# Attention over 32 heads: a hardware loop of four passes written out in a straight line

## The chip, the cores and the metric

The kernel runs on one core of a Trainium2 chip. The metric is the device time of one execution in microseconds (us), lower is better. A core has five engines that run their own instruction streams side by side and meet only at semaphores: TensorE (PE, matrix products), VectorE (DVE), ScalarE (ACT), GpSimd (POOL) and SyncE (SP, which here starts the transfers).

## The reference, cut to what matters

The reference is one decoder layer in float32: a state-space mixer, a grouped-query cross-attention over a context, a feed-forward part, each followed by a layer norm. Only the attention is touched:

```python
# b = 2, 16 heads in 4 groups, 512 queries, 1536 keys, head width 96
scores = jnp.einsum('bkgqd,bksd->bkgqs', q, k) * scale
attn = jax.nn.softmax(scores.astype(jnp.float32), axis=-1).astype(q.dtype)
out = jnp.einsum('bkgqs,bksd->bkgqd', attn, v)
```

## The kernel before, in words

The program has five phases, each with its own semaphores and buffers: `mamba_in`, `mamba_scan`, `project_norm_qkv`, `attention`, `attention_out_feed_forward`. A product in float32 is made of three matmuls on a high and a low part of each operand. q, k and v lie in DRAM when `attention` starts, and its result goes back to DRAM.

`attention` works through 2 x 16 = 32 heads (`hd`), in 8 groups of 4 heads that share k and v (`w` is the group, `g` the head in it, `s = w % 2` the buffer of k and v). In each head:

- PE makes 12 tiles of scores (`scores`, three matmuls each) of 128 keys by 512 queries into two PSUM banks in turn, so the scores of tile t wait for the exponential of tile t - 2. Between them it makes the products with v (`values`, three matmuls, four tiles behind, `LAG`), the products from which the next head's maxima are read (`maximum`, 4 x 3 matmuls), and at t = 10 four short transposes (`transposes`).
- ACT, for each tile, takes the exponential from PSUM (L1455) and copies it to the high part (L1458). At t = 6 it splits the query of the head after next (L1443), at six places of heads g = 1 and g = 2 it splits a piece of the next group's k or v (L1436, L1439), and at t = 10 it copies the row of maxima (L1448), once per head.
- POOL makes the low part of each exponential (L1552). DVE reduces the maxima (L1497), divides by the sums (L1504, L1510) and makes the low parts of q, k and v. SP loads k, v and q and stores the result.

All five engines run this through one helper, `heads` (L1383): a loop of `NW // 2 = 4` passes over a body in which 2 groups, 8 heads, are written out. Each engine has a loop of its own, with its own counter register `j`; no engine waits for another at the turn from one pass to the next. Inside the body every number that depends on the head, in a wait or in a transfer's address, is computed from `j`:

```python
        with eng.Fori(0, NW // 2) as j:
            for s in range(2):
                for g in range(G):
                    body(2 * G * j + G * s + g, 2 * j + s, g, s)
```

Before the loop, PE, ACT and DVE do the first head's maxima, its query and the first k and v; after it the last four tiles, the last division and the last store follow.

Of the kernel before, what the change touches and what calls it, by code (L numbers as in the profile page):

```python
# [34 lines left out]
G = NH // KV  # L35
# [1286 lines left out]
def attention(nc, res, d):  # L1322
# [18 lines left out]
    NW = B * KV  # L1341
# [40 lines left out]

    def heads(eng, body):  # L1383

        with eng.Fori(0, NW // 2) as j:
            for s in range(2):
                for g in range(G):
                    body(2 * G * j + G * s + g, 2 * j + s, g, s)

    SET, POOL_SET = 5, 2 + 2 * LAG  # L1390
    SPLIT_AT = ((1, 4), (1, 7), (1, 10), (2, 1), (2, 4), (2, 9))
# [1 line left out]
    with nc.Block() as block:  # L1393
        @block.sync
        def _(sp):
# [23 lines left out]
            sp.wait_ge(q_lo_done, 1)  # L1419
            load_q(2, 0)  # L1420
            heads(sp, body)
            store(NHD, 0)
            sp.wait_ge(on_st[0], 16 * (NHD // 2 + 1))
# [6 lines left out]
        def _(act):  # L1430
# [44 lines left out]
            row(0, 0)  # L1475
            act.wait_ge(before_done, 1)
            heads(act, body)

        @block.vector
        def _(dve):  # L1480
# [58 lines left out]
            maximum(0, 3)  # L1539
            queries(1, 1)  # L1540
            heads(dve, body)
            reciprocals(NHD, 0)
            divide(NHD, 0)
# [625 lines left out]
```

## Time and profile before

| | us |
|---|---|
| median of 3 runs (lowest, highest) | 3586.15 (3581.65, 3586.78) |
| profiled execution, its own time | 3582.83 |
| its span, first to last instruction | 3581.5 |
| the loop over heads in it, about | 1768 to 2422 |
| 41307 instructions; PE busy | 3221.2 (90%) |

The own time of the profiled execution is 1.3 us more than its span. The loop over heads is 654 us of the span, 18%. Its four passes can be told apart in the trace because ACT copies the row of maxima (L1448) once per head, and because the loop's own instructions stand under line 1385: a register operation at the head of each pass, and an addition and a compare-and-branch at its end.

### The profile page before, as it was taken

The numbers are of one execution on the slowest core, as the hardware profiler recorded it, in microseconds if no ns is written. First come the engines' busy times: TensorE is split into PE (matmuls) and PEld (weight loads), VectorE is DVE, ScalarE is ACT, GpSimd is POOL, SyncE is SP. The second block draws the span as 40 slices with busy tenths as digits, with TensorE's granted clock in tenths as the row PEclk, the third lists the DMA queues.
The fourth block names the chain that finished last, engine by engine and source line by source line (L and its number), as shares of the span: only waits on it lengthen the run. The fifth ranks groups of instructions, "written<-read, shape, count | busy, mean of one in ns | idle before, by whom it ended". The sixth has DMA issues, their size and how long they took to land. (4 is left out here: it accounts for less than half of the span.)

```text
span 3581.5 us, 41307 instructions
## 1 busy us (share of the span) xinstructions
PE 3221.2 (90%) x12763; PEld 2387.8 (67%) x12763; DVE 2195.0 (61%) x1925; ACT 1512.5 (42%) x2148; POOL 1399.2 (39%) x794
## 2 busy tenths in 40 slices
PE   9999777878777689999799999997889999999996
PEld 7877433333332267898587878786668888888884
DVE  6554499999999946621377777774644333333426
ACT  4447644444444432411387888782321122121111
POOL 0002299999999823000287878780100000000001
PEclk9999889999999999999899999999999999999998
DMA  3124531113110076422211111115211111111101
GB/s 110 41 80 165 184 128 62 45 50 139 50 62 31 15 252 208 144 80 94 76 32 32 35 31 35 31 33 199 78 65 47 41 59 53 35 53 53 47 18 59
DMA packets 125427, 273.15 MB, mean 76 GB/s; under 512 B 24448, under 2 KB 38656, under 8 KB 122400
## 3 DMA queue, kind: packets, MB, share of 16 engines
q1 hardware_dynamic: 107632, 262.42, 21.7%
q10 hardware_dynamic: 17712, 9.79, 0.9%
q8 instruction: 32, 0.52, 0.1%
q14 instruction: 51, 0.42, 0.0%
HBM read 207.87 MB, written 64.29 MB: 76 GB/s over the span
## 5 line engine op out<-in xcount | busy, mean ns | idle before, releaser
L799 PE MATMUL scan_ps_y<-scan_g,scan_ident 128*128 128x512 f32 x1024 | 518.8, 640 | 189.5 <-DVE scan_g L730 172.8
L771 POOL TENSOR_TENSOR scan_dbx<-scan_u,scan_b_bc 128x1024 f32<-128x1024 f32 x256 | 594.2, 2355 | 31.6 <-DMA scan_b_bc<-bc 31.6
L1552 POOL TENSOR_TENSOR at_p_lo<-at_p,at_p_hi 128x512 fp32r<-128x512 f32 x384 | 515.7, 1350 | 159.5 <-ACT at_p_hi L1458 149.1
L702 ACT ACTIVATE scan_ps_a<-scan_dt,scan_a_neg 128x512 f32<-128x512 f32 x512 | 328.0, 679 | 442.6 <-DVE scan_g L730 435.7
L799 PEld LDWEIGHTS scan_ps_y<-scan_g,scan_ident 128*128 128x128 f32 x1024 | 193.2, 199 | 482.5 <-DVE scan_g L730 296.0
L927 POOL TENSOR_TENSOR ff_y<-ff_y,ff_rstd 128x512 f32<-128x512 f32 x14 | 24.9, 1806 | 1124.1 <-DVE ff_rstd L916 1124.1
L743 DVE TENSOR_TENSOR_SCAN scan_ps_a<-scan_ps_a,scan_dbx 128x512 f32<-128x512 f32 x384 | 441.5, 1210 | 1.5 <-POOL scan_dbx L771 1.5
L1497 DVE TENSOR_REDUCE at_neg_max<-at_ps_mx 128x1 fp32r<-128x1536 f32 x132 | 232.0, 1758 | 164.3 <-PE at_ps_mx L1572 152.4
L1972 DVE TENSOR_TENSOR ff_hf<-ff_sg,ff_ps_u 128x1024 f32<-128x1024 f32 x28 | 34.2, 1221 | 388.2 <-PE ff_ps_u L97 388.2
L1455 ACT ACTIVATE at_p<-at_ps_s 128x512 f32<-128x512 f32 x384 | 227.8, 593 | 104.7 <-PE at_ps_s L1589 86.6
L1458 ACT ACTIVATE at_p_hi<-at_p 128x512 fp32r<-128x512 f32 x384 | 242.8, 632 | 12.2
L730 DVE TENSOR_TENSOR scan_g<-scan_ps_a,scan_c_bc 128x1024 f32<-128x1024 f32 x192 | 231.1, 1204 | 0.0
L95 PE MATMUL in_ps<-in_x_hi,in_w_hi 128*128 128x512 f32 x512 | 202.2, 395 | 0.0
L96 PE MATMUL in_ps<-in_x_lo,in_w_hi 128*128 128x512 f32 x512 | 200.7, 392 | 0.0
L97 PE MATMUL in_ps<-in_x_hi,in_w_lo 128*128 128x512 f32 x512 | 200.4, 391 | 0.0
L95 PE MATMUL ff_ps_g<-ff_x_hi,ff_w_hi 128*128 128x512 f32 x448 | 176.3, 394 | 5.7 <-DVE ff_x_lo L1912 5.7
L96 PE MATMUL ff_ps_g<-ff_x_lo,ff_w_hi 128*128 128x512 f32 x448 | 175.3, 391 | 0.0
L97 PE MATMUL ff_ps_g<-ff_x_hi,ff_w_lo 128*128 128x512 f32 x448 | 175.0, 391 | 0.0
L95 PE MATMUL ff_ps_u<-ff_x_hi,ff_w_hi 128*128 128x512 f32 x448 | 174.8, 390 | 0.0
L97 PE MATMUL ff_ps_y<-ff_h_hi,ff_w_lo 128*128 128x512 f32 x448 | 174.5, 389 | 0.0
L96 PE MATMUL ff_ps_y<-ff_h_lo,ff_w_hi 128*128 128x512 f32 x448 | 174.4, 389 | 0.0
L97 PE MATMUL ff_ps_u<-ff_x_hi,ff_w_lo 128*128 128x512 f32 x448 | 174.4, 389 | 0.0
(253 smaller groups left out, 7201.3 us busy)
## 6 DMA issues: line engine op xcount, KB each, us to landing
ff_w<-in_w SPq DMA_DIRECT2D x56, 512.0 KB, 4.2
in_w<-in_w_in SPq DMA_DIRECT2D x32, 512.0 KB, 3.6
mid_w<-in_w_out SPq DMA_DIRECT2D x32, 512.0 KB, 4.8
ff_w<-in_w SPq DMA_DIRECT2D x56, 256.0 KB, 2.6
ff_wo_wo<-in_w_o SPq DMA_DIRECT2D x32, 384.0 KB, 3.1
scan_cx<-in_ctx SPq DMA_DIRECT2D x9, 1024.0 KB, 5.7
sz<-in_xz SPq DMA_DIRECT2D x16, 512.0 KB, 3.0
dt<-in_acc SPq DMA_DIRECT2D x16, 512.0 KB, 3.6
```

Of the source, the lines that this page charges most:

```text
L95: nc.tensor.matmul(out, w_hi, x_hi, start=start, stop=False)
L96: nc.tensor.matmul(out, w_hi, x_lo, start=False, stop=False)
L97: return nc.tensor.matmul(out, w_lo, x_hi, start=False, stop=stop)
L702: nc.scalar.activation(ps_a[(2 * s + k) % SB][:, h], dt[s][:], ACT.Exp, scale=a_neg[:, it, 2 * k + h:2 * k + h + 1]).then_inc(a_ready, 1)
L730: nc.vector.tensor_tensor(g[s][:], ps_a[s][:], c_bc[:, 2 * k:2 * k + 2], ALU.mult).then_inc(g_ready, 1)
L743: nc.vector.tensor_tensor_scan(out[:, h], ps_a[slot][:, h], dbx[k % SL][:, h], 0.0, ALU.mult, ALU.add).then_inc(scanned, 1)
L771: nc.gpsimd.tensor_tensor(dbx[k % SL][:], u[s][:].unsqueeze(1).to_broadcast([P, 2, L]), b_bc[:, 2 * k:2 * k + 2], ALU.mult).then_inc(dbx_r ...
L799: last = nc.tensor.matmul(ps_y[:], ident[:], g[(2 * s + k) % SB][:, h], start=False, stop=k == NK - 1 and h == 1)
L1455: nc.scalar.activation(p[t % NSL][:], ps_s[t % 2][:], ACT.Exp, scale=SCALE).then_inc(exp_done, 1)
L1458: nc.scalar.activation(p_hi[t % NSL][:], p[t % NSL][:], ACT.Copy).then_inc(p_hi_done, 1)
L1497: nc.vector.tensor_reduce(neg_max[:, i, HD:HD + 1], ps_mx[:].rearrange("p n l -> p (n l)"), AX_X, ALU.max, negate=True).then_inc(max_done, 1)
L1552: nc.gpsimd.tensor_tensor(p_lo[t % NSL][:], p[t % NSL][:], f32(p_hi[t % NSL][:]), ALU.subtract).then_inc(p_lo_done, 1)
```

## The change

The helper `heads` no longer opens a loop. It calls the body 32 times, in the same order and with the same arguments as plain numbers; `s` is now `w % 2`. Nothing else is changed: the same data instructions in the same order on each engine, with the same semaphores and the same values waited for.

```diff
     def heads(eng, body):
 
-        with eng.Fori(0, NW // 2) as j:
-            for s in range(2):
-                for g in range(G):
-                    body(2 * G * j + G * s + g, 2 * j + s, g, s)
+        for w in range(NW):
+            for g in range(G):
+                body(G * w + g, w, g, w % 2)
 
     SET, POOL_SET = 5, 2 + 2 * LAG
```

## Rows read from the trace of the kernel before

**Rows 1.** The page: busy time and share of the span; the instruction queues (packets, MB, share).

```profile
PE 3221.2 (90%) x12763; PEld 2387.8 (67%) x12763; DVE 2195.0 (61%) x1925; ACT 1512.5 (42%) x2148; POOL 1399.2 (39%) x794
...
q8 instruction: 32, 0.52, 0.1%
q14 instruction: 51, 0.42, 0.0%
```

**Rows 2.** Windows, busy us: length, PE, PEld, DVE, ACT, POOL, then PE clock, DMA, GB/s.

```profile
1768.00:2422.00 654.00, 646.79 (x2828) 522.48 (x2828) 480.74 (x304) 525.48 (x884) 515.71 (x384) 0.99 0.12 33
```

**Rows 3.** Waits in 1768 to 2422: us in total, times, longest.

```profile
ACT L1455 <- issue: 8.5, 3, 3.3
...
PE at_ps_s L1587 <- ACT at_p L1455: 6.1, 3, 2.5
```

**Rows 4.** Timeline of the first turn, 1930 to 1937: start us, length, engine, line.

```profile
1930.91 0.63 ACT L1458 ACTIVATE at_p_hi<-at_p 128x512 fp32r<-128x512 f32 x1
1931.11 0.40 PE L1589 MATMUL at_ps_s<-at_q_hi,at_k_lo 96*128 96x512 f32 x1
...
1934.85 1.28 ACT L1455 ACT_TABLE_LOAD   x1 [3.31 <-issue]
1936.15 0.60 ACT L1455 ACTIVATE at_p<-at_ps_s 128x512 f32<-128x512 f32 x1
1936.78 0.63 ACT L1458 ACTIVATE at_p_hi<-at_p 128x512 fp32r<-128x512 f32 x1
...
1936.80 0.50 PE L1587 MATMUL at_ps_s<-at_q_hi,at_k_hi 97*128 97x512 f32 x1 [2.50 <-ACT at_p L1455]
```

**Rows 5.** Line 1385 in 1924 to 1938: sequencer, operation, ns, first and last start.

```profile
L1385 PEldq COMPARE_BRANCH  x1: 208/208/208, 1927.8 to 1927.8; - x1
L1385 PEldq FUSED_REGOPS  x1: 50/50/50, 1928.1 to 1928.1; - x1
...
L1385 ACTq COMPARE_BRANCH  x1: 45/45/45, 1931.0 to 1931.0; - x1
...
L1385 ACTq FUSED_REGOPS  x1: 66/66/66, 1934.7 to 1934.7; - x1
```

**Rows 6.** Line 281, the first phase's loop of 8 passes: operation, count, ns min/median/max.

```profile
L281 ACT ACT_TABLE_LOAD  x8: 1283/1283/1283, 28.3 to 200.3; - x8
```

**Rows 7.** Windows right behind the first and the second turn, columns as in Rows 2.

```profile
1937.00:1940.60 3.60, 3.60 (x10) 2.83 (x10) 0.02 (x1) 2.63 (x5) 3.11 (x3) 0.55 0.00 0
2100.20:2104.00 3.80, 3.80 (x17) 3.11 (x18) 1.52 (x1) 3.53 (x7) 3.21 (x3) 1.00 0.00 0
```

**Rows 8.** Timeline of PE at the second and the third turn.

```profile
2100.11 0.50 PE L1587 MATMUL at_ps_s<-at_q_hi,at_k_hi 97*128 97x512 f32 x1 [1.57 <-ACT at_p L1455]
...
2262.31 0.50 PE L1587 MATMUL at_ps_s<-at_q_hi,at_k_hi 97*128 97x512 f32 x1 [2.00 <-ACT at_p L1455]
```

**Rows 9.** Timeline of ACT, line 1448 of heads 0, 3, 4, 7, 8, 15, 16, 23, 24.

```profile
1789.63 0.59 ACT L1448 ACTIVATE at_q_hi<-at_ps_t 1x512 fp32r<-1x512 f32 x1
...
1849.70 0.59 ACT L1448 ACTIVATE at_q_hi<-at_ps_t 1x512 fp32r<-1x512 f32 x1
1869.60 0.59 ACT L1448 ACTIVATE at_q_hi<-at_ps_t 1x512 fp32r<-1x512 f32 x1
...
1929.66 0.59 ACT L1448 ACTIVATE at_q_hi<-at_ps_t 1x512 fp32r<-1x512 f32 x1
1953.89 0.59 ACT L1448 ACTIVATE at_q_hi<-at_ps_t 1x512 fp32r<-1x512 f32 x1
...
2093.90 0.59 ACT L1448 ACTIVATE at_q_hi<-at_ps_t 1x512 fp32r<-1x512 f32 x1
2115.64 0.59 ACT L1448 ACTIVATE at_q_hi<-at_ps_t 1x512 fp32r<-1x512 f32 x1
...
2255.64 0.59 ACT L1448 ACTIVATE at_q_hi<-at_ps_t 1x512 fp32r<-1x512 f32 x1
2277.84 0.59 ACT L1448 ACTIVATE at_q_hi<-at_ps_t 1x512 fp32r<-1x512 f32 x1
```

## The prediction

> **What bounds the kernel now.** I read the page first [rows 1]: PE is busy 90% of the span, no other engine over 61%, so a gain has to come out of time in which PE stands still or runs slow. The change touches only the loop over heads, so the second view is the windows for that stretch [rows 2]: in 654.0 us PE is busy 646.8, with the granted clock at 0.99 on the mean. PE is idle there for 7.2 us; that is nearly all that anything done to this loop can give back, beside what a slow clock costs.
>
> The third view is the waits of the same stretch [rows 3]. Of the 7.2 us, 6.1 are three waits of PE for the exponential on ACT, and ACT itself has three stretches, 8.5 us in all, in which it waits for nothing the profile shows ("issue"). Three is the number of turns of a loop of four passes.
>
> The fourth is the timeline of the first turn [rows 4]. The scores of the next tile are done on PE at 1931.11 + 0.40 = 1931.51, and ACT ends its last copy at 1930.91 + 0.63 = 1931.54, so the exponential could start at once. Instead ACT is idle for 3.31 us, then loads its activation table for 1.28 us, and the exponential starts at 1936.15: 4.6 us late. PE goes on with what it has, then stands 2.50 us for it, because the scores have two banks. The loop's own instructions say what the 3.31 us are [rows 5]: ACT's compare-and-branch is at 1931.0, the first instruction of the next pass at 1934.7, 3.7 us later. PE's branch (1927.8 to 1928.1) costs 0.3 us, while its engine still has matmuls queued.
>
> **The change part by part.**
>
> (1) *The turn of ACT goes*, three times: idle time of 8.5 us in all [rows 3] and no branch. The Trainium skill, "Runtime: NRT & Kernel Launch", section "Instruction fetch mechanics", says that a taken branch to a target outside the two pages held has to fetch it before going on, and that code in a row is fetched ahead, mostly hidden. The 3.7 against 0.3 us of [rows 5] fits that, if ACT's body doesn't fit and PE's does.
>
> (2) *Three of the four table loads go.* The exponential needs its table; inside a pass there is one load for 96 exponentials and 96 copies, so nothing in the body drives it out. The load is at the head of each pass because the state on entry isn't known there. The first phase shows the same rule: 8 passes, 8 loads [rows 6]. In a straight line only the first one is needed, and it lies beside PE's first scores already. That is 3 x 1.28 = 3.8 us of ACT.
>
> (3) *What PE gets back.* ACT's 8.5 + 3.8 = 12.3 us are not the sum, since PE has some cover. I take the sum from steps between equal points of successive heads [rows 9]. With no turn between them, head 3 to head 4 (the first of a group, like those behind a turn) takes 1869.60 - 1849.70 = 19.90 us. Across the turns it takes 24.23, 21.74 and 22.20. The excess is 4.33, 1.84 and 2.30 us, together 8.47.
>
> The parts agree with PE's side: its idle time is 2.50, 1.57 and 2.00 [rows 4, 8], 6.07 together, plus the start of the first matmul behind a gap. At the first turn there is one thing more: from 1937.0 to 1940.6 the granted clock is 0.55 and PE starts 10 matmuls in 3.6 us; behind the second turn it is 1.00 with 17 in 3.8 us [rows 7]. So behind the 2.50 us gap the clock fell to its 1.2 GHz level, behind 1.57 it stayed at 2.4. That costs 3.6 x 0.45 = 1.6 us and is inside the 4.33. With no gap there, it goes too.
>
> (4) *The turns of PE, DVE, POOL and SP go.* PE's costs 0.3 us of its sequencer [rows 5] and runs ahead of the matmuls. The scores that PE ends at 1931.51 [rows 4] belong to the next pass already, so PE is past its turn before ACT is; it is ACT that PE meets later. Price 0. Once ACT no longer stalls, next late would be POOL or DVE, but inside the passes they hold PE up nowhere that counts: 1.1 us is all PE's idle time outside the turns.
>
> (5) *Register arithmetic becomes constants.* Two waits and a computed value stand between an exponential and its copy, and the copy at 1936.78 starts 0.03 us behind the exponential's end (1936.15 + 0.60) [rows 4]. The arithmetic is done while the engine works. Lower bound of the gain 0; upper bound the 2.9 us worked out under rival C. I take 0, nearest to the 0.03 us row. A loss has no place: instructions only go away.
>
> (6) *More code is fetched*, once each, in place of a body that is run four times. Both instruction queues move 0.94 MB now, at 0.1% of the DMA engines [rows 1], beside a DMA share of 0.12 in the loop [rows 2]; bandwidth is no issue. Whether the fetch keeps ahead can be read off the first pass, which already runs all 8 heads as new code on all engines: heads 0 to 7 take 1929.66 - 1789.63 = 140.03 us there, and 2093.90 - 1953.89 = 140.01 and 2255.64 - 2115.64 = 140.00 in the second and third pass [rows 9], in which PE, DVE, POOL and SP run what they may still hold. New code costs 0.02 us per pass or nothing. Lower end 0; upper end, if each block were waited for, a turn's price of 1.84 to 4.33 us per stall. I take 0.
>
> (7) *Before and after the loop.* The first matmuls of the loop and the last tiles stay as they are; leaving the loop costs no jump. The last phase starts 8.5 us earlier as a whole. Price 0.
>
> **Sum.** 3582.83 - 8.47 = 3574.4 us for the profiled execution. Its time is 3.3 us below the median of the three runs, so for the median I expect 3586.15 - 8.47 = 3577.7, and say 3577. What one can tell from no change here is about 0.2%, 7.2 us; the forecast is only just over it, which is why "same" gets a good share.
>
> **The rivals.**
>
> *A. The fetch stays, only the loads go.* If ACT's buffer is refilled at the same rate in a straight line, it would meet a stall of some 3 us at three places anyway. Then 1.28 us per turn is taken off ACT, and PE's gaps of 2.50, 1.57 and 2.00 shrink by that much: 3.84, and 1.6 for the clock, since a gap of 1.2 is less than the 1.57 that left it alone. Gain 5.4 us at most, median 3581. For it: the idle is put down to no one. Against: the first pass crosses the same code with no such stall.
>
> The Trainium skill, "ScalarE: Activation LUTs", section "What ACT_TABLE_LOAD costs", gives a load 1283 ns, which the row has to the digit, and a drain of 1380 ns beside it. By that, part of the 3.31 us would be the load's and rival A would come out at 3 x 2.66 = 8.0 us off ACT, near the forecast.
>
> *B. A straight line that runs dry (slower).* Place: ACT, in front of an exponential, in the 24 heads of the passes that used to be repeats. ACT makes 884 / 32 = 28 operations a head [rows 2] with several waits beside each. Price: a stall of 3 us costs PE 1.84 to 4.33 us, mean 2.8. With one in each head: 24 x 2.8 = 67 us, less 8.5: 3645. It decides from 4 stalls on (4 x 2.8 = 11 > 8.5); to be slower by 0.2% it takes 6. Against: none in the 8 heads of the first pass.
>
> *C. The constants help as well.* The seven steps inside a pass take 140.03 us where seven of 19.90 would take 139.3 [rows 9]: 0.7 us a pass is lost in heads in which ACT has k and v to split beside its tiles. If register work is in that chain, up to 4 x 0.7 = 2.9 us more go: 3574.8. Against: the 0.03 us between ACT's operations [rows 4], which leaves next to nothing for it.
>
> *D. The loads aren't taken out*, or the loop is rebuilt in some way: ACT would be late by 1.28 us at most, about what PE's banks cover. Gain about 6 to 8.5 us; it ends inside the forecast's range.
>
> **How the numbers follow.** Forecast with D 0.78 (gain 6.5 to 10.5, median 3575.6 to 3579.7, plus some 2 us for the median of few runs); A 0.10; C 0.08; B 0.04. Faster by over 0.2% needs 3579.0 or less: most of the forecast (0.64 of its 0.78) and C: 0.72. Same: the rest of the forecast, and A: 0.24. Slower: B, 0.04. Range 3570 to 3584: C and the lower runs below, A and the higher runs above; B is left out.
>
> **What would show it.** In the profile after: one table load on L1455 in place of four; no "issue" idle time on ACT; no wait of PE for ACT's exponential over 0.5 us; steps across the old turns of 19.9 us; granted clock 1.00 at heads 8 and 9; seven steps inside a group of 8 heads of 140.0 us, as before; more MB on the instruction queues. New "issue" time on ACT or PE in the later heads would show A or B, seven steps well below 140.0 us C. The prediction is wrong if the steps come down and the total doesn't: something behind the loop would then have taken the time.

## The result, and the profile after

The changed kernel takes 3569.72 us (median of 5 runs, 3568.72 to 3573.32) against 3586.15 (5 runs timed beside it), so the two medians differ by 16.4 us. The ratio of the comparison, which isn't the quotient of the two medians, is 0.9959, 95% interval 0.9945 to 0.9974, that is 14.7 us less (9.3 to 19.7); gains "by the ratio" below are worked out in the same way. The direction is as forecast. The size is not: 8.5 us were forecast, and the median lies just under the range's low end of 3570. The profiled execution went from 3582.83 to 3573.32 us, 9.5 less, so profile and timed runs disagree by 5 us or more on the gain. Some 2 us of that disagreement turned out to be the lesson of this case; the rest stays open.

The page after, to be held against [rows 1]: the same matmuls, about as busy, and more code on one of the instruction queues.

```profile
PE 3217.1 (90%) x12763; PEld 2386.3 (67%) x12763; DVE 2197.4 (62%) x1925; ACT 1509.4 (42%) x2145; POOL 1400.5 (39%) x794
...
q8 instruction: 49, 0.80, 0.1%
q14 instruction: 48, 0.39, 0.0%
```

The table loads on the exponential's line (count, ns, first and last start), then the windows over the whole loop, columns as in [rows 2]. There is one load where there were four. PE is idle for 1.5 us in 646 where it was idle for 7.2 in 654, and the granted clock is 1.00 on the mean.

```profile
L1454 ACT ACT_TABLE_LOAD  x1: 1283/1283/1283, 1767.6 to 1767.6; - x1
```

```profile
1765.00:2411.00 646.00, 644.48 (x2829) 521.48 (x2828) 480.98 (x305) 523.02 (x882) 516.71 (x384) 1.00 0.12 34
```

The waits of the loop, to be held against [rows 3]: no wait of a PE matmul for ACT's exponential and no "issue" time on ACT are left.

```profile
POOL at_p_lo L1551 <- ACT at_p_hi L1457: 137.9, 201, 26.6
ACT at_p L1454 <- PE at_ps_s L1588: 85.3, 118, 1.1
...
PEld at_ps_s L1586 <- ACT at_q_hi L1447: 3.7, 8, 0.5
ACT L1454 <- PE at_ps_s L1588: 1.8, 1, 1.8
```

The row copies at heads 7 and 8, 15 and 16, 23 and 24, which answer to those of [rows 9]: each step is 19.89 us, where it was 24.23, 21.74 and 22.20.

```profile
1926.99 0.59 ACT L1447 ACTIVATE at_q_hi<-at_ps_t 1x512 fp32r<-1x512 f32 x1
1946.88 0.59 ACT L1447 ACTIVATE at_q_hi<-at_ps_t 1x512 fp32r<-1x512 f32 x1
...
2086.72 0.59 ACT L1447 ACTIVATE at_q_hi<-at_ps_t 1x512 fp32r<-1x512 f32 x1
2106.61 0.59 ACT L1447 ACTIVATE at_q_hi<-at_ps_t 1x512 fp32r<-1x512 f32 x1
...
2246.45 0.59 ACT L1447 ACTIVATE at_q_hi<-at_ps_t 1x512 fp32r<-1x512 f32 x1
2266.34 0.59 ACT L1447 ACTIVATE at_q_hi<-at_ps_t 1x512 fp32r<-1x512 f32 x1
```

From head 0 to head 31 that makes 619.04 us (1787.14 to 2406.18) where the kernel before had 628.24: 9.20 less. Of these, 8.50 are the three steps; 0.7 come from the third head of each group, 19.82 in place of 19.90 us. The first head is 0.34 shorter. Outside the loop the new profile is 2.2 us ahead when the loop begins and gives 2.1 back after it; those parts run the same instructions, and in the twelve profiles taken in all the start of the loop (first row copy) lies anywhere from 1761.5 to 1767.3 us.

### The profile page after: what moved, and what is told of

Read it like the earlier page. It is cut to its first block and busy times, and to the rows that moved or that the text cites. A ratio compares the mean times of both kernels' runs of the same rounds, so it can differ in the third digit from the quotient of the medians.

```text
span 3571.9 us, 39359 instructions
## 1 busy us (share of the span) xinstructions
PE 3217.1 (90%) x12763; PEld 2386.3 (67%) x12763; DVE 2197.4 (62%) x1925; ACT 1509.4 (42%) x2145; POOL 1400.5 (39%) x794
## 5 line engine op out<-in xcount | busy, mean ns | idle before, releaser
L96 PE MATMUL ff_ps_u<-ff_x_lo,ff_w_hi 128*128 128x512 f32 x448 | 174.3, 389 | 0.0
L95 PE MATMUL ff_ps_y<-ff_h_hi,ff_w_hi 128*128 128x512 f32 x448 | 174.3, 389 | 0.0
```

The lines of the kernel that those rows point to most:

```text
L95: nc.tensor.matmul(out, w_hi, x_hi, start=start, stop=False)
L96: nc.tensor.matmul(out, w_hi, x_lo, start=False, stop=False)
```

## The experiments

**The two halves, and the change again.** `heads` got a switch, and each engine either keeps the loop or is written out; the diff shows the half with ACT alone.

```diff
-    def heads(eng, body):
+    def heads(eng, body, straight=False):
+        if straight:
+            for w in range(NW):
+                for g in range(G):
+                    body(G * w + g, w, g, w % 2)
+            return
+        with eng.Fori(0, NW // 2) as j:
...
-            heads(act, body)
+            heads(act, body, straight=True)
```

> The changed kernel once more, timed side by side with the one before. The profiles of the first pair differ by 9.6 us, of which 9.5 lie in the loop over heads; the medians differ by 16.4 us. Theory (the gain is the loop's and the rest is scatter of the parts around it): the ratio comes nearer to 1 - 9.5/3586 = 0.9974, a median some 8 to 13 us under before, and in the profile again steps of 19.89 us across the old turns and about 619.0 us from the row of head 0 to that of head 31 (before: 628.2). Rival (something outside the loop gained as well): again 14 us or more, with a stretch outside the loop that is shorter in every profile.

Measured: 3571.47 us, ratio 0.9961 (0.9947 to 0.9974). Steps across the old turns 19.90, 19.89 and 19.89, head 0 to head 31 619.05 us. The loop repeats to 0.01 us. The gain, 14.0 us by the ratio and 13.5 between the medians, repeats as well, so the scatter theory isn't enough.

> Only ACT's loop is written out; PE, DVE, POOL and SP keep their loops of four passes. Theory (the three turns of ACT, fetch and table load, are the gain): steps across the turns of 19.9 us, loop from head 0 to head 31 about 619.7 us, that is 8.5 under before, total like the changed kernel within 1 us. Rival (turns or register arithmetic of the other engines count too): the steps across the turns stay above 20.5 us or every step is longer than in the changed kernel, total 3 us or more above it. The 0.08 us by which every third head of a group got shorter (19.90 to 19.82) tells whose constants gave it: 19.82 here if ACT's, 19.90 if another engine's.

Measured: 3572.24 us, ratio 0.9959 (0.9946 to 0.9973), loop 619.69 us. With ACT alone written out the steps across the turns are 19.91, 19.92 and 19.88, so nearly the whole gain is ACT's. The third heads stay at 19.90: their 0.08 us is not ACT's.

> The opposite half: PE, DVE, POOL and SP are written out, ACT keeps its loop of four passes. Theory: ACT's turns are still there, three stretches of 2.4 to 3.3 us with a table load of 1.28 us behind each, the steps across them 21.7 to 24.2 us, the loop 628 us, total within 1 us of before (0.7 us less if the 0.08 us per third head are not ACT's). Rival (the turns of all engines share the loss): a gain of 2 us or more.

Measured: 3577.68 us, ratio 0.9980 (0.9971 to 0.9989). In the loop the theory holds: 628.68 us, steps of 23.69, 21.57 and 24.06 across the turns, ACT's branch at 1927.9 and its next instruction at 1931.1. The third heads have their 19.82. But the total is 7 us under before (4 to 10), where 1 was expected, and its own profile shows no place for it in the loop. That was a miss. The 7 us don't add up with the rest either: in the same comparison ACT alone gave 14.7 us by the ratio and everything together 14.0, so on top of ACT the other engines' straight code gave nothing that can be told.

**The kernel before against itself, and PE alone.** The miss called for a test of the measurement.

> The kernel before against itself. In the timed runs every variant so far came out some 4 to 8 us shorter than its loop over heads explains: even the one whose ACT loop is as before (loop 628.7 us against 628.2) has a median of 3577.7 against 3585.0. Theory 1 (this is the measurement: which program comes first on a chip, or where it lies): the same kernel shows a ratio near 0.998, 4 to 8 us. Theory 2 (real, outside the loop): ratio 1.000 within its interval, medians 3583 to 3587, and its profile has the loop at 628 us and about 1767 us before it.

Measured: 3583.41 us over 11 runs, ratio 0.9994 (0.9985 to 1.0003): no difference that can be told, with single runs from 3576.7 to 3588.3. The first theory, that the measurement gives the second kernel 4 to 8 us, isn't borne out; a real gain outside the loop isn't excluded by this. Its profile answered another question. The row copies of the same six heads:

```profile
1928.32 0.59 ACT L1448 ACTIVATE at_q_hi<-at_ps_t 1x512 fp32r<-1x512 f32 x1
1952.67 0.59 ACT L1448 ACTIVATE at_q_hi<-at_ps_t 1x512 fp32r<-1x512 f32 x1
...
2092.70 0.59 ACT L1448 ACTIVATE at_q_hi<-at_ps_t 1x512 fp32r<-1x512 f32 x1
2116.37 0.59 ACT L1448 ACTIVATE at_q_hi<-at_ps_t 1x512 fp32r<-1x512 f32 x1
...
2256.40 0.59 ACT L1448 ACTIVATE at_q_hi<-at_ps_t 1x512 fp32r<-1x512 f32 x1
2279.78 0.59 ACT L1448 ACTIVATE at_q_hi<-at_ps_t 1x512 fp32r<-1x512 f32 x1
```

The steps are 24.35, 23.67 and 23.38, an excess over 19.90 of 11.7 us where the first profile had 8.5; the loop was expected at 628 us and took 631.5. ACT was no later than before: its idle time in front of the table loads is 3.44, 2.75 and 2.46 us (before: 3.31, 2.38, 2.84). PE's waits sum to 6.2 us (6.1). What differs is the clock behind the gaps. The windows of 3.6 us right behind each turn, columns as in [rows 2]; first the kernel before run again, then the third turn of the first profile:

```profile
1936.00:1939.60 3.60, 3.60 (x11) 2.79 (x10) 0.28 (x1) 2.42 (x5) 3.33 (x3) 0.53 0.00 0
2099.70:2103.30 3.60, 3.60 (x11) 2.83 (x10) 0.43 (x1) 2.41 (x5) 3.34 (x3) 0.55 0.00 0
2263.10:2266.70 3.60, 3.60 (x12) 2.79 (x11) 0.75 (x1) 2.42 (x5) 3.33 (x3) 0.61 0.00 0
```

```profile
2262.70:2266.30 3.60, 3.60 (x17) 2.94 (x16) 1.60 (x1) 3.32 (x7) 3.31 (x3) 1.00 0.00 0
```

In the second execution the granted clock fell to its 1.2 GHz level behind all three gaps, the shortest 1.65 us long; in the first it fell behind one, and stayed at 2.4 GHz behind one of 2.00 us.

> Only PE's loop is written out. The forecast's price is 0: PE's turn costs 0.3 us of its sequencer behind queued matmuls. If the 7 us of the variant with all but ACT written out belong to PE's code, this one shows them too (median 3577 to 3579, ratio 0.998); if they belong to DVE, POOL or SP, or are the measurement's, it is at 3583 to 3587 or as the kernel before is against itself. Inside the loop: steps of 19.82 in place of 19.90 us for the third head of a group if that came from PE's constants, 19.90 if not; turns as before.

Measured: 3581.97 us, ratio 0.9990 (0.9981 to 0.9999). The third heads are at 19.81 to 19.84, so PE's constants give the 0.08 us (0.7 in all). The turns are 24.25, 24.37 and 23.48, with the clock down behind all three. Of the 7 us of the half before, this shows at most a part: 3.6 us by the ratio (0.4 to 6.8).

With that there are four profiles in which ACT keeps the turns. For each turn: PE's wait for the exponential, the excess of the step over 19.90 us, and the granted clock in the 3.6 us (3.8 for one) behind the wait.

| Profile | First turn | Second turn | Third turn |
|---|---|---|---|
| before | 2.50, 4.33, 0.55 | 1.57, 1.84, 1.00 | 2.00, 2.30, 1.00 |
| before, again | 2.60, 4.45, 0.53 | 1.94, 3.77, 0.55 | 1.65, 3.48, 0.61 |
| PE alone written out | 2.53, 4.35, 0.59 | 2.64, 4.47, 0.54 | 1.76, 3.58, 0.62 |
| all but ACT written out | 1.96, 3.79, 0.62 | 1.41, 1.67, 1.00 | 2.33, 4.16, 0.55 |

Where the clock fell, the excess is 1.82 to 1.85 us more than the wait; where it stayed up, 0.26 to 0.30. So a fall costs some 1.55 us at each turn, and nine of the twelve turns have one.

**A table load without the branch.**

```diff
+    other = [sb(f"other{s}", [1, 1]) for s in range(3)]
...
                     act.wait_ge(p_lo_done, n + 1)
+                    if (g, t) == (0, 0) and w in (2, 4, 6):
+                        nc.scalar.activation(other[w // 2 - 1][:], ident[0:1, 0:1], ACT.Sqrt)
                     nc.scalar.activation(p[t % NSL][:], ps_s[t % 2][:], ACT.Exp, scale=SCALE).then_inc(exp_done, 1)
```

> The changed kernel, in which ACT at the three old turns (heads 8, 16 and 24, first tile) takes a square root of one element into a scratch cell, so that its table is changed and changed back: two table loads and no branch. It prices the loads apart from the fetch. From the three turns of before, PE's loss is ACT's delay less about 1.8 us of cover (4.59, 3.66 and 4.12 us late; 2.66, 1.75 and 2.17 lost between matmul starts, the 1.6 us of the slow clock apart). Theory (a load costs its 1.28 us and nothing beside): ACT is late by 2 x 1.28 + about 0.2 = 2.8 us, PE loses 0.9 to 1.0 us at each place, together 2.8 us over the changed kernel, with the granted clock at 1.00. Rival by the Trainium skill, ScalarE: Activation LUTs, What ACT_TABLE_LOAD costs (a drain of 1380 ns beside each load): 2 x 2.66 + 0.2 = 5.5 us late, PE loses 3.7 us at each place, 11 us or more over the changed kernel. Third: a single load of 1.28 us, as at the turns, lies wholly inside the cover of 1.8 us, so of the gain of 8.5 us the fetch alone would be 3 us plus the clock, and neither cause alone all of it.

Measured: 3572.69 us, ratio 0.9964 (0.9950 to 0.9977); the steps at the three places are 20.87, 20.88 and 20.88, so 0.98 us is lost at each. The timeline at head 8, ACT and PE:

```profile
1926.55 1.28 ACT L1456 ACT_TABLE_LOAD   x1
...
1928.06 1.28 ACT L1457 ACT_TABLE_LOAD   x1
...
1929.35 0.60 ACT L1457 ACTIVATE at_p<-at_ps_s 128x512 f32<-128x512 f32 x1
...
1930.00 0.50 PE L1589 MATMUL at_ps_s<-at_q_hi,at_k_hi 97*128 97x512 f32 x1 [0.72 <-ACT at_p L1457]
```

Two loads stand back to back with the square root between them, 1.51 us from start to start, and PE waits 0.72 us (0.71 at the other two places); behind all three gaps the clock stayed up. That is the 0.9 to 1.0 us of the theory. The Trainium skill, "ScalarE: Activation LUTs", section "What ACT_TABLE_LOAD costs", gives a drain of 1380 ns beside a load's 1283. The load's length agrees, but no such drain adds to it in this case: by an estimate from the two figures PE would have lost 3.7 us at each place, and 0.98 was measured. It also follows that a single load of 1.28 us is under PE's cover of 1.8 us.

**A shorter body for ACT's loop.** Everything is as in the kernel before, but ACT makes 8 passes of 4 heads in place of 4 passes of 8. The buffer of v's high part is changed like that of k's.

```diff
-    k_hi = [sb(f"k_hi{s}", [HD + 1, S], F32R) for s in range(2)]
+    k_hi_both = sb("k_hi", [HD + 1, 2, S], F32R)
+    k_hi = [k_hi_both[:, s] for s in range(2)]
...
-                    nc.scalar.activation(k_hi[s][0:HD, c], k[:, c], ACT.Copy).then_inc(kv_hi_done, 1)
+                    nc.scalar.activation(k_hi_both[0:HD, s, c], k[:, c], ACT.Copy).then_inc(kv_hi_done, 1)
...
-                        split_kv(w + 1, 1 - s, SPLIT_AT.index((g, t)))
+                        split_kv(w + 1, (w + 1) % 2, SPLIT_AT.index((g, t)))
...
-            heads(act, body)
+            with act.Fori(0, NW) as w:
+                for g in range(G):
+                    body(G * w + g, w, g, w % 2)
```

> The kernel before, all loops kept, but ACT's loop has 8 passes of one group in place of 4 passes of two: half the body, 270 instructions in place of 540 in the trace, 7 turns in place of 3, and 8 table loads. (The buffer of the next k and v is chosen by a register on ACT.) Theory (the body of 540 does not fit what the engine holds, so a turn waits for code; 270 fits): the branch costs 0.3 us at each of the 7 turns, each with a load of 1.28 us behind it, 1.6 us late is under the cover of 1.8 us, PE never waits for ACT over 0.3 us, steps across the turns 19.9 us, loop from head 0 to head 31 about 619.7 us as with ACT alone written out, total 10 us or more under before. Rival (a turn or a load costs the same whatever the body's length, or a taken branch always waits): 7 turns with PE losing 1.8 to 4.5 us each, the loop 631 to 650 us, slower than before by 4 to 16 us.

Measured: 3573.59 us over 8 runs, ratio 0.9973 (0.9963 to 0.9984), a gain of 9.7 us by the ratio and 10.6 between the medians. The loop takes 619.73 us: the same as with ACT written out (619.69), with seven turns in it. The first of them, line 1479 being ACT's loop, then ACT's timeline there:

```profile
L1479 ACTq COMPARE_BRANCH  x1: 45/45/45, 1845.1 to 1845.1; - x1
L1479 ACTq FUSED_REGOPS  x1: 71/71/71, 1845.4 to 1845.4; - x1
```

```profile
1845.07 0.63 ACT L1460 ACTIVATE at_p_hi<-at_p 128x512 fp32r<-128x512 f32 x1
1845.72 1.28 ACT L1457 ACT_TABLE_LOAD   x1
1847.02 0.60 ACT L1457 ACTIVATE at_p<-at_ps_s 128x512 f32<-128x512 f32 x1
```

The branch at 1845.1 is followed by the next pass at 1845.4, as on the other engines, and the table load starts 0.02 us behind the last copy. The exponential is at 1847.02, 1.3 us late, and PE has no wait for it. The rival (a turn costs the same whatever the body's length) fell: it gave 631 to 650 us.

**Moving the pieces of k and v.** In the written-out kernel, and then in the one with the short loop.

```diff
-    SPLIT_AT = ((1, 4), (1, 7), (1, 10), (2, 1), (2, 4), (2, 9))
+    SPLIT_AT = ((1, 2), (1, 4), (1, 8), (2, 1), (2, 4), (2, 8))
```

> The changed kernel with the pieces of the next k and v moved to other tiles on ACT: heads 1 of a group at t = 2, 4, 8 in place of 4, 7, 10, heads 2 at t = 1, 4, 8 in place of 1, 4, 9, so that none lies beside the row copy at t = 10. Theory (the 20.42 us of heads 1 against 19.73 to 19.9 of the others is ACT's split at t = 10 in front of the row, which makes one exponential late): these steps fall to 19.8 us or so, 8 x 0.6 = 4.8 us less than the changed kernel. Rival (PE waits there for something else, as the transposes or the clock): the steps stay 20.4 us.

Measured: 3568.24 us, ratio 0.9950 (0.9936 to 0.9963), the lowest median of all. All steps are now 19.87 to 19.93, head 0 to head 31 616.71 us, 2.3 less than the changed kernel and not 4.8. The 20.42 did fall, but the 19.73 of the fourth heads rose to 19.89: part of the long step was only a late row copy, which the next steps gave back. A step between two copies on ACT is not time of PE; a sum over a group is.

> The same short ACT loop with the pieces of k and v moved to other tiles (heads 1 at t = 2, 4, 8, heads 2 at 1, 4, 8). Theory: the two add up, the loop at 617 to 618 us (the written-out kernel with the pieces moved: 616.7), total within 2 us of that one's median of 3568, with a fraction of its code. Rival (the load at each group's first tile and the moved pieces together use up ACT's cover): steps above 20 us in heads 0 or 1 of a group.

Measured: 3570.64 us, ratio 0.9959 (0.9946 to 0.9973), loop 616.73 us. The two add up in the loop.

> The changed kernel a third time, beside the two above. Theory: the turns of before cost 8.5, 11.7, 12.4 and 9.7 us in the four profiles that have them, 10.6 on the mean; with the 0.7 us of the third heads the loop gains 11.3 us on the mean, and the total 11 to 14 us (the kernel before against itself came out 1.9 us apart, interval 0 to 5). Rival (the written-out code gains outside the loop too): more than the kernel with the short ACT loop by 3 us or more, beyond the 0.7 us of the constants.

Measured: 3572.47 us, ratio 0.9965 (0.9952 to 0.9979), loop 619.18 us. That is 12.5 us of gain by the ratio (11.8 between the medians). Against the kernel with the short loop it is 1.1 us less by the medians and 2.9 by the ratios, whose intervals overlap; the rival asked for 3 beyond the 0.7 of the constants, and isn't borne out.

## Why the prediction came out as it did

- **What bounds the loop, and step 1, ACT's turn: right.** The half with ACT alone gives the gain, the other half keeps the turns. The cause given for the 3.7 us, code that isn't held, is borne out by the short body: counted in the trace of before, a pass is 539 instructions on ACT, and from its branch to the next pass's first instruction it takes 2.8 to 3.7 us; with 277 it takes 0.3. PE's pass has 1605 (704 matmuls, 704 weight loads, 197 of its sequencer), POOL's 290, DVE's 178, SP's 66, and there it takes 0.2 to 0.4 us. In the program's other loops ACT has at most 158 instructions a pass, and between passes it takes at most 0.27 us. The pages show the fetching itself: queue q14 moved 51 packets before, 41 with ACT written out and 32 with ACT's short loop, while q8 stayed at 32 packets in all three. So ACT's long loop moved more code than the same work in a straight line. The Trainium skill, "Runtime: NRT & Kernel Launch", section "Instruction fetch mechanics", gives a buffer of 512 instructions, on PE 2048; the trace agrees, ACT's body being the only one above its figure. On ACT nothing between 277 and 539 instructions was run, so no run shows where the step lies.
- **Step 2, the loads: counted right, worth nothing alone.** One load is left of four. But a load with no fetch in front of it lies under PE's cover: seven of them cost nothing in the short loop. In the turn the two causes add up to 3.5 to 4.7 us late and share one cover of 1.8. So a load's price depends on what stands in front of it: behind a fetch that stays, as in rival A, it would by the same sum still cost its 1.28 us (no run has that case), and with the fetch gone it costs nothing. Rival D left it up to 2.5 us.
- **Step 3, the sum: the step that failed, in one term.** It took 8.47 us from three turns of a single execution. The four profiles that have the turns show excesses of 8.5, 11.7, 12.4 and 9.6 us, 10.6 on the mean. PE's idle time hardly differs (5.7 to 6.9 us, mean 6.2, where 6.07 was taken); the term that was mis-sized is the slow clock. It was counted once (1.6 us), and the prediction explained by the length of the gap why it came at 2.50 and not at 1.57 us. Over the twelve turns it came nine times, behind gaps of 1.65 to 2.64 us, and not behind 1.41, 1.57 and 2.00. So it is 3 x 0.75 x 1.55 = 3.5 us on the mean where 1.6 was taken. I read a rule into one case of each; what else decides it, no run here shows.
- **Step 4, the other engines' turns: right** inside the loop, price 0.
- **Step 5, the constants: 0.7 us, not 0**, and PE's, not ACT's. It lies inside the bounds; rival C, which put up to 2.9 us on ACT's chain, had the wrong engine.
- **Step 6, the fetch of more code: right.** Seven steps within eight heads take 139.85, 139.84 and 139.84 us in the first three eights, and rivals A and B fell: ACT has no idle time without a cause in the loop. Queue q8 moved 0.28 MB more, and it did so with PE alone written out too; q14 moved 0.03 less.
- **Step 7 and the median.** 10.6 + 0.7 = 11.3 us are explained by the loop on the mean. By their ratios the three timed comparisons gave 14.7, 14.0 and 12.5 us. The profiled execution was forecast at 3574.4 us and took 3573.3; that this is so near is in part luck, since the stretches before and behind the loop differ by 1.5 to 2.8 us between executions of one kernel. The rest of the timed gain, 1.2 to 3.4 us, is within what the kernel before shows against itself (its interval runs from 1.1 us slower to 5.4 faster), and isn't settled. Nor are the 7 us of the half without ACT, whose interval (4 to 10) excludes both 0 and the 0.7 that its loop explains. No run here isolates where they lie.

## What to carry to other kernels

Before a hardware loop is blamed or unrolled, count the instructions of a pass on each engine and read the time from its branch to the next pass's first instruction: here only the engine whose body isn't held paid, and halving its body did as much in the loop as writing that engine out. Price a stall with the cover taken off once for all causes that meet there. And where PE goes cold behind a gap in one execution and not in the next, take the clock's cost from several executions, as a share of the gaps, not from the one profile at hand.

## What the runs showed of the hardware

- From the branch of the loop over heads to the next pass's first instruction it took 0.2 to 0.4 us for bodies of up to 290 instructions (1605 on PE), and 2.6 to 3.9 us on ACT for a body of 539 (four profiles); with 277 instructions it took 0.3 us on ACT too.
- The granted clock fell to its 1.2 GHz level behind nine of twelve gaps of 1.4 to 2.6 us on PE that had been busy before, behind one of 1.65 us and not behind one of 2.00, and cost 1.55 us each time.
- A table load took 1.283 us every time. It started 0.02 us behind the last activation at the forced loads and at the seven turns of the short loop, with no drain beside it.
- PE lost nothing to ACT being 1.3 us late, and 0.98 us to its being 2.8 us late: two PSUM banks and the work between gave it 1.8 us of cover.
